# Second batch's score stacks copied inside SBUF, its pieces cut by ScalarE and VectorE, and all engine orders rewritten

## The chip, the cores and the metric

The kernel runs on one core of a Trainium2 chip. The metric is the time of one execution on the device in microseconds (us). Before the change three executions took 1351.9, 1354.87 and 1353.01 us, median 1353.01. A profiled execution took 1353.93 us.

## The reference, cut to what matters

Eight sequences ("batches") of 512 tokens with 256 features pass through four blocks, each of the form `x = x + layernorm(block(layernorm(x)))`:

```python
c_kv = x @ W_kv_down                                  # attention, 16 heads of 16
k_rope = rotary(c_kv @ W_k_rope); q_rope = rotary(x @ W_q_rope)
k, v, q = c_kv @ W_k_up, c_kv @ W_v_up, x @ W_q
scores = (q . k per head + q_rope . k_rope) / sqrt(48), causal softmax, @ v, @ W_o
h = bitlinear(x, w_fc) + gate * (x @ v.T @ fast_b.T @ u.T)   # first dense block
y = bitlinear(relu(h) ** 2, w_proj)
z = conv(x @ W_in)                                    # mixer: 32 channels of decaying sums
num = cumsum(p_w * cos(k_val * theta)), cumsum(p_w * sin(k_val * theta)); den = cumsum(p_w)
y = silu(combine(num / den, q_raw)) @ W_out
y = relu(x @ W1 + b1) @ W2 + b2                       # second dense block
```

All is float32. The products of q and k are taken in bfloat16: q and k are each cut into three bfloat16 pieces whose sum is the float32 value, and six products of pieces are summed.

## The kernel before, in words

Work is cut into named items of four chains: `a` (attention), `d` (the dense blocks, and the projections that feed the mixer), `m` (the mixer) and `p` (preparing weights, once). `a1.S.0` stands for item `S`, number 0, of chain a in batch 1. The chains of neighbouring batches overlap: while batch 1 is in its attention, batch 0 is in its first dense block and then starts its mixer. `MERGE` is a table of numbers that says, per engine, how many items of which chain come next; it is the whole order of an engine. `BANKS` gives each result its PSUM bank in TensorE's order. Every engine runs its order strictly, and waits on semaphores.

The steps of attention that matter here: `ckv`, `q`, `k`, `qr`, `kr`, `v` are projections of the normalized input xT. `base` adds the causal mask to the rotary part of the scores. `S` is one unit of scores (of 40 in a batch): TensorE multiplies two "stacks" (L983), VectorE adds the base and finds the row minimum (L1486), ScalarE takes the exponential (L1241). `T` transposes the unit on TensorE (L991), ScalarE copies it out of PSUM (L1248; for batch 0 every second one VectorE, L1415). `PV` multiplies with the values (L1009), `OT` transposes the output back (L1018). Head group g uses units 10g to 10g+9 and stack g mod 2, so group 2's stack can be loaded only when TensorE has done unit 9, and group 3's when it has done unit 19.

A stack holds 96 partitions of pieces of q (and 96 of k), with each head's 16 features on its own 16 partitions. Pieces come out of the projections with another placement, so the stacks are filled by DMA, all of them issued by SyncE (SP):

- Batch 0: ScalarE casts q from PSUM (L1223), VectorE takes the rest (L1454), ScalarE casts the rest (L1227, item `cast`), VectorE takes what is left as the third piece (L1461). The pieces lie in `hid`, and per group 12 DMAs of 64 KB copy them SBUF to SBUF into the stack (L666).
- Batches 1 to 7: ScalarE casts, VectorE takes the rest (L1422), and GpSimd casts the rest and subtracts (L794, L796). Four DMAs of 384 KB write the pieces to a `scratch` in HBM (L722, item `pieces`), and per group six DMAs read them back (L672).

The first dense block: `fxT` and `zxT` transpose normalized tokens, `fc` (eight products, L905) and `fproj` (four, L914) are the matrix products, `fystats`, `zstats`, `fnorm`, `znorm` the layernorms, in which GpSimd takes the power -0.5 (L785) between two ScalarE passes (L1180, L1171). `z.2`, `z.0`, `z.1` are the projections for the mixer; `z.0` is convolved on VectorE (L1431), stored to HBM `values` (L734) and read back spread over the partitions (`kv`, L741). The mixer's `turn` (L1548) and `frac` (L1558) on VectorE write the halves of a `ring` of 8 slots; `fold` (L1303), `cos` (L1307), `sin` (L1310) on ScalarE; `scan` (L1567) and `mix` (L1576) on VectorE; `gather` (L1077) on TensorE. `frac` number 1 writes half slot 5 of the ring.

Of the kernel before, what the change touches and what calls it, by code (L numbers as in the profile page):

```python
# [67 lines left out]
def attention_items(b):  # L68

    if b == 0:  # L70
        items = ["ckv", ("q", 0), ("cast", 0), ("k", 0), ("cast", 1), "qr", ("group", 0), ("q", 1), ("cast", 2), "kr", ("k", 1), ("cast", 3)]
# [1679 lines left out]
```

## Time and profile before

| what | value |
|---|---|
| median of three executions | 1353.01 us |
| profiled execution | 1353.93 us |
| its span in the trace | 1352.1 us |
| TensorE (PE) busy | 1197.1 us, 89% |
| VectorE (DVE) busy | 1117.4 us, 83% |
| ScalarE (ACT) busy | 1055.3 us, 78% |
| GpSimd (POOL) busy | 253.3 us, 19% |
| DMA of 64 KB, SBUF to SBUF (batch 0) | 48 of them, 2.7 us to landing |
| DMA of 384 KB to scratch | 28 of them, 4.8 us |
| stack loads from scratch (192, 128 and 64 KB) | 168 of them, median 4.2 us |

The span begins with the first instruction, 1.8 us of the execution lie around it. Busy time is a share of the whole; what a change is worth is read where it sits, which is here from 109 us (the projections of batch 1) to about 230 us (the end of its attention).

### The profile page before, as it was taken

Reading aid. Unit: us, or ns where it says so; the run is one execution under the profiler, and the core shown is the slowest. Engines: PE = TensorE matmul, PEld = TensorE weight load, DVE = VectorE, ACT = ScalarE, POOL = GpSimd, SP = SyncE. Lnnn points to the kernel's source line nnn. Section 1 sums busy time; section 2 is a strip of 40 time slices with the busy share of each in tenths; the row PEclk is TensorE's granted clock in tenths of the full one; section 3 lists DMA queues with packets and bytes.
Section 4 is the critical chain, followed back from the end, with each engine's and each line's share of the span. In section 5 each row is a group of like instructions: output and inputs, shape, how many; then the busy total and the mean of one; then the engine's idle time right before and its main releaser. Section 6 shows DMA issues by size and latency. Waiting matters only on the chain.

```text
span 1352.1 us, 23241 instructions
## 1 busy us (share of the span) xinstructions
PE 1197.1 (89%) x8060; PEld 771.1 (57%) x8060; DVE 1117.4 (83%) x2343; ACT 1055.3 (78%) x2105; POOL 253.3 (19%) x245
## 2 busy tenths in 40 slices
PE   5999995899899999998999999999899988973867
PEld 2774764466565754675656664666565764641444
DVE  2983489999699979899889997999889998899930
ACT  5775799678978989799958989698969988648542
POOL 3952000310031004200131101401131001111011
PEclk9799996999999999999999999999999999986979
DMA  4603241514024125310451131612333131023000
GB/s 141 186 18 92 42 135 39 122 35 136 32 77 103 25 63 150 87 36 21 135 125 50 30 112 39 148 24 65 103 90 75 24 114 46 32 63 95 16 16 16
DMA packets 73171, 100.07 MB, mean 74 GB/s; under 512 B 10960, under 2 KB 45920, under 8 KB 73056
## 3 DMA queue, kind: packets, MB, share of 16 engines
q1 hardware_dynamic: 73056, 98.59, 27.1%
q8 instruction: 66, 1.08, 0.3%
q14 instruction: 49, 0.40, 0.1%
HBM read 71.29 MB, written 24.12 MB: 71 GB/s over the span
## 4 chain that ended last, share of the span: by engine, by line
PE 48%; DVE 22%; ACT 18%; issue 8%; POOL 2%; SPq 1%; DMA 1%; DVEq 0%; POOLq 0%; ACTq 0%
PE ps L905 17%; PE ps L914 13%; DVE work L1567 7%; PE ps L991 5%; DVE work L1486 4%; PE ps L1009 4%; ACT work L1241 3%; PE ps L983 3%; PE ps L1077 2%; ACT xnd L1180 2%; DVE work L1558 2%; ACT work L1248 2%; ACT xnd L1171 1%; DVE work L1548 1%; DVE work L1576 1%
## 5 line engine op out<-in xcount | busy, mean ns | idle before, releaser
L1567 DVE TENSOR_TENSOR_SCAN work<-work 128x512 f32<-128x512 f32 x256 | 307.8, 1234 | 28.4 <-ACT work L1307 26.8
L1241 ACT ACTIVATE work<-work 128x384 f32<-128x384 f32 (+3 forms) x512 | 266.4, 564 | 38.5 <-DVE work L1486 37.9
L785 POOL TENSOR_TENSOR later_norms<-later_norms,singles 128x2 f32<-128x2 f32 x112 | 104.7, 939 | 864.8 <-ACT xnd L1180 583.3
L1486 DVE CUSTOM_DVE_ANT_0 work<-ps,work 128x384 f32<-128x384 f32 (+3 forms) x512 | 224.7, 486 | 35.7 <-PE ps L983 31.6
L991 PE MATMUL ps<-ident,work 128*128 128x128 f32 x1280 | 199.9, 280 | 24.1 <-ACT work L1241 20.0
L991 PEld LDWEIGHTS ps<-ident,work 128*128 128x128 f32 x1280 | 150.4, 144 | 71.9 <-issue 46.8
L1248 ACT COPY work<-ps 128x512 f32<-128x512 f32 x300 | 171.7, 579 | 2.8 <-PE ps L991 2.7
L1576 DVE TENSOR_TENSOR work<-work 128x1024 f32<-128x1024 f32 x128 | 158.4, 1238 | 4.7 <-DVEq L1400 0.2
L983 PE MATMUL ps<-work 96*128 96x384 bf16 (+3 forms) x512 | 122.7, 308 | 2.4 <-DVE hid L1510 1.1
L905 PE MATMUL ps<-led_xTd,wf 128*128 128x512 f32 x256 | 118.1, 611 | 3.9 <-issue 3.0
L914 PE MATMUL ps<-wf,hid 128*128 128x256 f32 x512 | 116.1, 387 | 4.5 <-issue 4.5
L914 PE MATMUL ps<-wpr,hid 128*128 128x256 f32 x512 | 117.1, 385 | 3.2 <-issue 2.9
L905 PE MATMUL ps<-led_xTd,wfc 128*128 128x512 f32 x256 | 116.8, 598 | 0.9 <-DVE work L1486 0.6
L914 PEld LDWEIGHTS ps<-wf,hid 128*128 128x128 f32 x512 | 98.7, 195 | 21.0 <-issue 7.2
L914 PEld LDWEIGHTS ps<-wpr,hid 128*128 128x128 f32 x512 | 96.7, 192 | 18.2 <-issue 5.0
L1009 PE MATMUL ps<-work 128*32 128x128 f32 x2560 | 93.7, 285 | 10.7 <-ACT work L1248 9.5
L1303 ACT ACTIVATE work<-work 128x1024 f32<-128x1024 f32 x64 | 67.2, 1058 | 33.4 <-DVE work L1558 33.3
L1558 DVE SCALAR_TENSOR_TENSOR work<-work,smalls 128x512 f32<-128x512 f32 x128 | 91.2, 756 | 2.2 <-ACT work L1298 0.7
L1009 PEld LDWEIGHTS ps<-work 128*32 128x32 f32 x2560 | 68.7, 113 | 37.3 <-issue 34.0
L1077 PE MATMUL ps<-work,sel 128*32 128x512 f32 x512 | 65.3, 630 | 20.3 <-DVE work L1576 20.3
L905 PEld LDWEIGHTS ps<-led_xTd,wf 128*128 128x128 f32 x256 | 48.3, 195 | 60.9 <-issue 59.7
L905 PEld LDWEIGHTS ps<-led_xTd,wfc 128*128 128x128 f32 x256 | 46.5, 190 | 52.6 <-issue 48.9
(185 smaller groups left out, 1925.4 us busy)
## 6 DMA issues: line engine op xcount, KB each, us to landing
work<-values SPq DMA_DIRECT2D x64, 256.0 KB, 3.1
work<-ratios SPq DMA_DIRECT2D x64, 256.0 KB, 3.3
scratch<-work SPq DMA_DIRECT2D x28, 384.0 KB, 4.8
work<-scratch SPq DMA_DIRECT2D x56, 192.0 KB, 4.0
work<-scratch SPq DMA_DIRECT2D x56, 128.0 KB, 4.2
x_in<-x SPq DMA_DIRECT2D x8, 512.0 KB, 6.3
values<-work SPq DMA_DIRECT2D x16, 256.0 KB, 2.7
ratios<-work SPq DMA_DIRECT2D x32, 128.0 KB, 2.8
```

The lines of the kernel that those rows point to most:

```text
L785: g_.tensor_tensor(rstds[chain][:, tokens], spreads[chain][:, tokens], power[:, tokens], ALU.pow).then_inc(*rstd.one)
L905: i = mm(dst, l, r, start=j == 0, stop=j == len(pairs) - 1)
L914: i = mm(ps[:, bank(b, name), tt % 2 * D:(tt % 2 + 1) * D], lhs[:, j, tt * P:(tt + 1) * P], rhs[:, j, :], start=j == 0, stop=j == n_k - 1)
L983: i = mm(out_of(b, name)[:, at:at + nk], stack[0:SROWS, hg % 2, 0, j, qt * P:(qt + 1) * P], stack[0:SROWS, hg % 2, 1, j, 0:nk], start=True ...
L991: i = tr(ps[:, bank(b, name), t * P:(t + 1) * P], sc[:, n % 4, t * P:(t + 1) * P], ident[:])
L1009: i = mm(ps[32 * j:32 * j + 32, bank(b, f"PV{hg}"), qt * P:(qt + 1) * P], v_all[:, v0:v0 + 32], pt[:, (hg * UNITS + u) % 6, at + t * P:at ...
L1241: i = s_.activation(part_of, part_of, ACT.Exp, scale=-1.0, bias=nmax[:, row:row + 1])
L1248: s_.copy(pt[:, n % 6, 0:nk], out_of(b, name)[:, 0:nk]).then_inc(*drains(b, name))
L1486: i = v_.tensor_tensor_reduce(sc[:, n % 4, at:at + nk], out_of(b, name)[:, at:at + nk], base_of(qt), -SCORE_SCALE, BIG, ALU.add, ALU.min, ...
L1558: i = v_.scalar_tensor_tensor(ring[:, SIN_HALF[r], m, :], kvr[:, slot, :], turns[:, r, m:m + 1], whole[:, COS_HALF[r], m, :], ALU.mult, AL ...
L1567: v_.tensor_tensor_scan(ring[:, at, m, :], pwr[:, slot, :], ring[:, at, m, :], 0.0, ALU.mult, ALU.add).then_inc(*scanned.one)
L1576: v_.tensor_tensor(both, both, qc[:, half * MH:(half + 1) * MH], ALU.mult).then_inc(*mixed.one)
```

## The change

`EARLY = 2` sets how many batches take the path of batch 0; before it was one. So in batch 1 the item order of q and k becomes that of batch 0, the second and third piece of q and k are made by ScalarE (`cast`) and VectorE in place of GpSimd, `pieces` is gone (four writes of 384 KB), and the stacks come by 48 DMAs of 64 KB from SBUF in place of 24 loads from HBM. The pieces lie in the ring's slots 5 to 7, which the mixer of batch 0 uses next: `frac` 1 of batch 0 waits for all 48 DMAs. The rest of k lies in the second half of `x2`. `MERGE` and `BANKS` are rewritten as a whole for all batches.

```diff
+EARLY = 2
 def attention_items(b):
-    if b == 0:
+    if b < EARLY:
         items = ["ckv", ("q", 0), ("cast", 0), ("k", 0), ("cast", 1), "qr", ("group", 0), ("q", 1), ("cast", 2), "kr", ("k", 1), ("cast", 3)]
     else:
         items = ["ckv", ("q", 0), ("q", 1), ("pieces", 0), "qr", ("k", 0), ("k", 1), ("pieces", 1), "kr"]
...
 MERGE = {
     "pe":
-        "a8 p2 a2 p4 a28 p a10 p a9 p a13 p a4 p a22 p a5 p a2 p2 a6 p a14 d a d a d7 a8 d a6 d a10 d a5 d a d2 "
...
+        "a4 p2 a6 p4 a25 p a4 p a9 p a11 p a18 p a16 p a p a9 p2 a5 p a15 d a2 d9 a8 d a10 d a10 d a10 d2 a11 d3 "
...
-        first_pieces = [hid[:, 3 * k:3 * k + 3, :].bitcast(BF16).rearrange("p a (b t) -> p (a b) t", t=T)
-                        .rearrange("p (c s) t -> p c s t", s=3) for k in range(2)]
+        places = [[hid[:, 3 * k:3 * k + 3, :].rearrange("p a t -> p (a t)") for k in range(2)],
+                  [ring[:, 5:8].rearrange("p a m t -> p (a m t)")[:, 3 * k * T:3 * (k + 1) * T] for k in range(2)]]
+        first_pieces = [[w.bitcast(BF16).rearrange("p (c s t) -> p c s t", c=DC, s=3) for w in pair] for pair in places]
...
-        first_rest = [rest, hid[:, 6:8, :]]
+        first_rest = [[rest, hid[:, 6:8, :]], [rest, x2[:, 1].rearrange("p t d -> p (t d)").rearrange("p (c t) -> p c t", c=DC)]]
...
             def load_group(b, hg):
-                if b == 0:
+                if b < EARLY:
                     for kind in range(2):
-                        need(sp, third_piece, 0, 2 * (hg // 2) + kind + 1)
+                        need(sp, third_piece, b, 2 * (hg // 2) + kind + 1)
...
-                if item in ("q", "k") and b:
+                if item in ("q", "k") and b >= EARLY:
                     pieces, pick = (q_pieces, (1, 2)) if item == "q" else (k_pieces, (1, 0))
...
                     need(dve, rounded, b, r + 1)
+                    if b == 0 and r == 1:
+                        for i in range(2):
+                            need(dve, first_stacked[i], 1, first_stacked[i].per_batch)
```

ScalarE at the start of batch 1's attention, beside the layernorms of batch 0's first dense block. The two passes L1171 (after: L1172) on xnd are `fnorm` 0 and 1, L1164 (L1165) copies `fxT` out of PSUM, L1234 (L1235) copies `v`. Before:

```order
L1180 ACTIVATE xnd,later_norms<-x,singles 128x256 x4
L1223 CAST work<-ps 128x512 x2
L1171 ACTIVATE xnd<-x,later_norms 128x256 x2
L1230 CAST work<-ps 128x512 x2
L1164 COPY led_xTd<-ps 128x2x256
L1171 ACTIVATE xnd<-x,later_norms 128x256 x2
L1234 COPY work<-ps 128x32x16
L1164 COPY led_xTd<-ps 128x2x256
L1234 COPY work<-ps 128x32x16
L1263 ACTIVATE hid<-ps,singles 128x512 x7
```

After:

```order
L1172 ACTIVATE xnd<-x,later_norms 128x256 x2
L1224 CAST work<-ps 128x512
L1228 CAST work<-xna 128x512
L1231 CAST work<-ps 128x512
L1228 CAST work<-x 128x512
L1224 CAST work<-ps 128x512
L1165 COPY led_xTd<-ps 128x2x256
L1228 CAST work<-xna 128x512
L1231 CAST work<-ps 128x512
L1172 ACTIVATE xnd<-x,later_norms 128x256 x2
L1165 COPY led_xTd<-ps 128x2x256
L1228 CAST work<-x 128x512
```

`fnorm` 0 stands ahead of q, and four casts (L1228) are new; `fnorm` 1 stands behind three of them and both of k's casts.

TensorE before the mixer's projections of batch 0 in the middle of batch 1's attention. L897 (L898) on xnd is the second half of `zxT`, L1058 (L1059) is `z.2`, L905 (L906) on wz is `z.0`; L991 is `T`, L983 `S`. Before:

```order
L991 MATMUL ps<-ident,work 128x128 x4
L983 MATMUL ps<-work 128x384
L983 MATMUL ps<-work 128x128
L991 MATMUL ps<-ident,work 128x128 x4
L897 MATMUL ps<-ident,xnd 128x128 x4
L1018 MATMUL ps<-ident,work 128x128 x4
L983 MATMUL ps<-work 128x384
L983 MATMUL ps<-work 128x128
L991 MATMUL ps<-ident,work 128x128 x4
L983 MATMUL ps<-work 128x256 x2
L1058 MATMUL ps<-led_xTd,wzs 32x132 x8
L905 MATMUL ps<-led_xTd,wz 128x512 x2
```

After:

```order
L992 MATMUL ps<-ident,work 128x128 x4
L1010 MATMUL ps<-work 32x128 x16
L984 MATMUL ps<-work 128x256 x2
L992 MATMUL ps<-ident,work 128x128 x4
L984 MATMUL ps<-work 128x512
L992 MATMUL ps<-ident,work 128x128 x4
L984 MATMUL ps<-work 128x512
L898 MATMUL ps<-ident,xnd 128x128 x4
L1059 MATMUL ps<-led_xTd,wzs 32x132 x8
L906 MATMUL ps<-led_xTd,wz 128x512 x2
```

Before, `z.0` comes when TensorE has sent units S 0 to 18 and T 0 to 14; after, S 0 to 21 and T 0 to 17.

VectorE where the mixer of batch 0 begins. L1548 (L1549) is `turn` 0, L1558 (L1562) `frac` 0; each pair of L1486 (L1487) rows is one part of a unit of scores. Before:

```order
L1548 TENSOR_SCALAR work<-work,smalls 128x512 x2
L1486 ISA work<-ps,work 128x256
L1486 ISA work 128x1
L1486 ISA work<-ps,work 128x256
L1486 ISA work 128x1
L1486 ISA work<-ps,work 128x512
L1486 ISA work 128x1
L1486 ISA work<-ps,work 128x512
L1486 ISA work 128x1
L1486 ISA work<-ps,work 128x512
L1486 ISA work 128x1
L1558 SCALAR_TENSOR_TENSOR work<-work,smalls 128x512 x2
```

After:

```order
L1487 ISA work<-ps,work 128x384
L1487 ISA work 128x1
L1487 ISA work<-ps,work 128x128
L1487 ISA work 128x1
L1549 TENSOR_SCALAR work<-work,smalls 128x512 x2
L1487 ISA work<-ps,work 128x256
L1487 ISA work 128x1
L1487 ISA work<-ps,work 128x256
L1487 ISA work 128x1
L1562 SCALAR_TENSOR_TENSOR work<-work,smalls 128x512 x2
```

`turn` 0 moved from behind unit 28 to behind unit 27, and `frac` 0 from behind unit 32 to behind unit 28. ScalarE's first mixer instruction, `fold` 0, moved from behind unit 32 to behind T 25.

## Rows read from the trace of the kernel before

**Rows 1.** Busy time by stretch: start:end, length, each engine, clock, DMA share, GB/s.

```profile
122.40:139.00 16.60, 16.33 (x49) 7.59 (x48) 7.87 (x18) 5.49 (x9) 1.37 (x1) 1.00 0.90 210
139.00:163.30 24.30, 23.66 (x187) 19.77 (x187) 10.21 (x41) 18.40 (x42) 1.40 (x2) 1.00 0.16 33
163.30:186.00 22.70, 20.39 (x217) 14.14 (x216) 17.01 (x61) 21.10 (x50) 1.40 (x2) 1.00 0.32 71
186.00:204.00 18.00, 14.79 (x149) 9.85 (x147) 17.14 (x53) 17.74 (x31) 0.00 (x0) 1.00 0.53 175
204.00:230.50 26.50, 15.64 (x138) 10.72 (x138) 23.48 (x45) 25.25 (x41) 1.01 (x1) 0.61 0.14 44
```

**Rows 2.** Waits of TensorE, 122 to 186 us: total, times, longest.

```profile
PE ps L897 <- ACT xnd L1171: 2.1, 1, 2.1
PE ps L991 <- ACT work L1241: 0.6, 2, 0.4
PE ps L983 <- DMA work<-scratch: 0.3, 1, 0.3
```

**Rows 3.** In order of time, batch 1's projections: start, length, engine, what, [idle before].

```profile
118.90 0.66 PE L897 MATMUL ps<-ident,xnd 128*128 128x128 f32 x4
...
122.42 12.25 PE L905 MATMUL ps<-led_xTd,wfc 128*128 128x512 f32 x28
...
117.40 0.91 ACT L1171 ACTIVATE xnd<-x,later_norms 128x256 f32<-128x256 f32 x2 [1.72 <-POOL later_norms L785]
...
120.08 0.91 ACT L1171 ACTIVATE xnd<-x,later_norms 128x256 f32<-128x256 f32 x2
```

**Rows 4.** Batch 0's second cast and third piece, by line: ns min/median/max.

```profile
L1227 ACT CAST hid<-xna x2: 603/611/619, 24.9 to 32.2; 128x512 bf16<-128x512 f32 x2
...
L1461 DVE TENSOR_TENSOR hid<-hid x2: 694/853/1012, 29.5 to 37.5; 128x512 bf16<-128x512 f32 x2
```

**Rows 5.** Batch 0's stack DMAs: SyncE's time for one issue in ns; us to landing.

```profile
L666 SPq DMA_DIRECT2D work<-hid x48: 547/594/754, 26.5 to 71.6; - x48
...
DMA to landing us min/median/max: 2.4/2.7/7.5
```

**Rows 6.** TensorE in order of time: a PV, unit 19, two transposes.

```profile
174.14 1.09 PE L1009 MATMUL ps<-work 128*32 128x128 f32 x32
175.16 0.39 PE L983 MATMUL ps<-work 96*128 96x256 bf16 x2
175.39 0.60 PE L991 MATMUL ps<-ident,work 128*128 128x128 f32 x4
...
176.05 0.60 PE L991 MATMUL ps<-ident,work 128*128 128x128 f32 x4
```

**Rows 7.** SyncE in order of time, the first stores and loads of the mixer.

```profile
180.52 0.34 SPq L734 DMA_DIRECT2D values<-work  x1
181.97 2.62 SPq L745 DMA_DIRECT2D ratios<-work  x4
184.64 2.58 SPq L741 DMA_DIRECT2D work<-values  x4
```

**Rows 8.** VectorE in order of time, start of the mixer, and one unit of ScalarE.

```profile
189.68 0.88 DVE L1548 TENSOR_SCALAR work<-work,smalls 128x512 int32<-128x512 f32 x2
...
197.10 1.41 DVE L1558 SCALAR_TENSOR_TENSOR work<-work,smalls 128x512 f32<-128x512 f32 x2
...
190.39 0.91 ACT L1241 ACTIVATE work<-work 128x256 f32<-128x256 f32 x2
191.20 0.57 ACT L1248 COPY work<-ps 128x512 f32<-128x512 f32 x1
```

**Rows 9.** A stretch of the start with its clock, and TensorE's wait ahead of it.

```profile
35.00:40.00 5.00, 5.00 (x17) 4.12 (x17) 4.01 (x9) 2.87 (x4) 5.00 (x6) 0.50 0.73 187
...
33.91 3.65 PE L1122 MATMUL ps<-work 16*128 16x256 f32 x8 [2.07 <-ACT work L1352]
```

**Rows 10.** Waits from 230 us to the end: total, times, longest.

```profile
ACT work L1303 <- DVE work L1558: 33.3, 18, 5.8
```

More of the change, by code:

```diff
@@ L73, in attention_items @@
         items = ["ckv", ("q", 0), ("q", 1), ("pieces", 0), "qr", ("k", 0), ("k", 1), ("pieces", 1), "kr"]
-    items += [("v", 0), ("v", 1), ("base", 0), ("base", 1), ("base", 2), ("base", 3), "fetch"] + [("group", 0)] * (b > 0) + [("group", 1)]
+    items += [("v", 0), ("v", 1), ("base", 0), ("base", 1), ("base", 2), ("base", 3), "fetch"] + [("group", 0)] * (b >= EARLY) + [("group", 1)]
     after = b + 1 < B
@@ L480, in sandwich_kernel @@
         third_piece = signal("third_piece", 2 * DC)
-        pieces_sent = signal("pieces_sent", 4, 16, 4 * (B - 1))
+        pieces_sent = signal("pieces_sent", 4, 16, 4 * (B - EARLY))
         n_stack = 2 * 2 * len(RUNS)
-        stacked = [signal(f"stack{i}_loaded", n_stack, 16, n_stack * (B - 1)) for i in range(2)]
-        first_stacked = [signal(f"first_stack{i}_loaded", 0, 16, 2 * 2 * SROWS // HD) for i in range(2)]
+        stacked = [signal(f"stack{i}_loaded", n_stack, 16, n_stack * (B - EARLY)) for i in range(2)]
+        first_stacked = [signal(f"first_stack{i}_loaded", 2 * 2 * SROWS // HD, 16, EARLY * 2 * 2 * SROWS // HD) for i in range(2)]
         exped = signal("exped", ALL)
@@ L666, in load_group @@
                             sp.dma_start(stack[k * HD:(k + 1) * HD, i, kind].rearrange("p j t -> p (j t)"),
-                                         first_pieces[kind][hg % 2 * 64:hg % 2 * 64 + 64, hg // 2, s, :]).then_inc(*first_stacked[i].one)
+                                         first_pieces[b][kind][hg % 2 * 64:hg % 2 * 64 + 64, hg // 2, s, :]).then_inc(*first_stacked[i].one)
                     return
@@ L716, in do @@
                     load_x(b + 1)
-                if item == "pieces" and b:
+                if item == "pieces":
                     need(sp, third_piece, b, (n + 1) * DC)
@@ L724, in do @@
                 if item == "group":
-                    if n < 2 and b:
-                        need(sp, pieces_sent, b - 1, 4)
+                    if n < 2 and b >= EARLY:
+                        need(sp, pieces_sent, b - EARLY, 4)
                     if n >= 2:
@@ L1222, in do @@
                     is_filled(act, b, f"q{n}")
-                    s_.copy((q_pieces if b else first_pieces[0])[:, n, 0, :], out_of(b, f"q{n}")).then_inc(*first_piece.one)
-                if item == "cast" and b == 0:
+                    s_.copy((q_pieces if b >= EARLY else first_pieces[b][0])[:, n, 0, :], out_of(b, f"q{n}")).then_inc(*first_piece.one)
+                if item == "cast":
                     c, kind = n // 2, n % 2
                     is_drained(act, b, f"{'qk'[kind]}{c}")
-                    s_.copy(first_pieces[kind][:, c, 1, :], first_rest[kind][:, c, :]).then_inc(*second_piece.one)
+                    s_.copy(first_pieces[b][kind][:, c, 1, :], first_rest[b][kind][:, c, :]).then_inc(*second_piece.one)
                 if item == "k":
                     is_filled(act, b, f"k{n}")
-                    s_.copy((k_pieces if b else first_pieces[1])[:, n, 2, :], out_of(b, f"k{n}")).then_inc(*first_piece.one)
+                    s_.copy((k_pieces if b >= EARLY else first_pieces[b][1])[:, n, 2, :], out_of(b, f"k{n}")).then_inc(*first_piece.one)
                 if item == "v":
@@ L1450, in do @@
                     copied(b, "ckv", ckv, out_of(b, "ckv"))
[L1451 removed]
+                if item in ("q", "k") and b < EARLY:
                     kind, of = ("q", "k").index(item), (0, 2)[item == "k"]
[L1453 to L1454 removed]
+                    need(dve, first_piece, b, 2 * n + kind + 1)
+                    v_.tensor_tensor(first_rest[b][kind][:, n, :], out_of(b, f"{item}{n}"), first_pieces[b][kind][:, n, of, :], ALU.subtract
                                      ).then_inc(*drains(b, f"{item}{n}"))
[L1456 removed]
+                if item == "q" and b >= EARLY:
                     split(b, "q", n, q_pieces[:, :, 0], 0)
[L1458 removed]
+                if item == "cast":
                     c, kind = n // 2, n % 2
                     need(dve, second_piece, b, n + 1)
[L1461 removed]
+                    v_.tensor_tensor(first_pieces[b][kind][:, c, (2, 0)[kind], :], first_rest[b][kind][:, c, :], first_pieces[b][kind][:, c, 1, :],
                                      ALU.subtract).then_inc(*third_piece.one)
@@ L1466, in do @@
                     rotate(b, "qr", qrope, T // 2)
-                if item == "k" and b:
+                if item == "k" and b >= EARLY:
                     split(b, "k", n, k_pieces[:, :, 2], DC)
```

46 lines of the change are left out of this document (20 added, 26 removed), and 75 rows, old and new, of the table MERGE.

## The prediction

> **What bounds the kernel now.** I read the page's busy shares first (the table above): TensorE 89%, VectorE 83%, ScalarE 78%. No engine stands out enough to be the only bound, so I asked for busy time by stretch over the place of the change [rows 1]. Three regimes show. From 122.4 to 139 us TensorE is full (16.33 of 16.60 us) with the `fc` products while VectorE works 7.87 us and ScalarE 5.49. From 139 to 163.3 TensorE is full (23.66 of 24.30) and ScalarE has 5.9 us to spare. From 163.3 to 230.5 ScalarE is full: 21.10 of 22.70, 17.74 of 18.00 and 25.25 of 26.50 us, 64.1 of 67.2; VectorE joins it from 186 us (17.14 of 18.00), and TensorE has 10.9 us idle in the last stretch and its granted clock is 0.61 there, so it runs at the lower of its two levels, 1.2 GHz, for most of it. So an early microsecond is gained only where TensorE idles before 163 us, and a late one only if ScalarE and VectorE get their work sooner. Third view, TensorE's waits from 122 to 186 us [rows 2]: 2.1 us for the second half of `zxT`, 0.6 us for exponentials, 0.3 us for a stack load. The last is all that batch 1's trip through HBM costs in waiting: the first unit of scores stands behind seven of eight `fc` products anyway. The change's headline step is thus worth 0.3 us, and the rest must come from what the order makes of it.
>
> **The change part by part.**
>
> *Pieces.* Four casts go to ScalarE and four subtractions to VectorE; eight instructions leave GpSimd. From batch 0's rows [rows 4] they cost 4 x 0.61 = 2.4 us on ScalarE and 4 x 0.85 = 3.4 us on VectorE (bounds 4 x 0.69 and 4 x 1.01). They lie in 113 to 123 us. TensorE has its projections to do there and both engines have gaps, so the cover is TensorE; if it were gone, the 3.4 us would count. One thing sticks out: `fnorm` 0 no longer waits for GpSimd (1.72 us, [rows 3]) as it moves ahead of q, but `fnorm` 1 now stands behind three new casts and k's second cast. I lay out ScalarE: `fxT` 0 is ready at about 119.4 (TensorE does the same products as before up to it, 118.90 + 0.5), then its copy 0.5, cast 0.5, k 0.5, `fnorm` 1 0.8, which ends near 121.8; before, the pass started at 120.08 and ended near 120.9. TensorE needs 0.5 for the transposes, ScalarE 0.6 for the copy, so the first `fc` starts at about 123.1 instead of 122.42 [rows 3]: a loss of 0.7 us, bounds 0 and 1.5.
>
> *Stacks.* SyncE issues 48 copies of 0.594 us (28.5 us) in place of 24 loads and four stores [rows 5]. Group 0: the third piece of q is there at about 116, of k at about 118.5; six issues each (3.6 us) end near 122.5, landed 2.7 us later, 125. The group 1 copies end near 130, landed 133. TensorE wants the first unit at about 139. Group 3 may be issued when unit 19 is done; 12 x 0.594 + 2.7 = 9.8 us later it is there. TensorE has 14 to 16 us of listed work between units 19 and 30 (T 16 to 26 and S 20 to 29 at 0.66 a pair, three `PV` of 1.02 [rows 6], `zxT`, the `z` products and two `query` products of four matmuls, 0.44 each by [rows 3]), so about 5 us of slack. I cost the stacks at nothing, the cover being TensorE's own work; what goes is the 0.3 us. The Trainium skill, page "DMA: Bandwidth & Descriptors", section "Rules for kernel authors", speaks against this edit: many small transfers should be joined into a large one, and under 64 KB it is mostly overhead. The trace has both kinds: a 64 KB copy lands in 2.7 us, a load from scratch in 4.2 at the median (the table), so the rule holds for SyncE's time and not for the latency that is waited for here; by the rule the slack of 5 us at unit 30 is where it would bite.
>
> *The added wait.* `frac` 1 of batch 0 waits for the last of the 48 copies. Before, `frac` 1 ran at 197.10 [rows 8]; unit 19 was done near 175.4 [rows 6], and the copies would be in by 185.2. Slack 12 us: nothing. Behind it in VectorE's queue stand `turn` 2 and units 33 on, so past that point each microsecond would count in full.
>
> *The order from 123 to 175 us.* `fproj` products now stand ahead of T 0, behind unit 8, T 9 and T 13, and the second `zxT` comes three units later. A filler of 3.5 us stands wherever TensorE would need fresh exponentials. I take the waits of [rows 2] as gone: -2.1, -0.6, -0.3. Bounds: all kept, 0; all gone, -3.0. With the 0.7 lost ahead this puts TensorE 2.3 us ahead at `z.0`, but `z.0` has three more units and a `PV` in front, 3 x 0.66 + 1.02 = 3.0 us [rows 6]. `z.0` is therefore 0.7 us later in absolute time (bounds 0 and 2).
>
> *From `z.0` to the end of batch 1's attention.* ScalarE decides [rows 1]. It has done three units more when `z.0` comes: 3 x 1.28 = 3.8 us (0.81 from start to start and 0.47 for the copy's part, [rows 8]) of the work that filled it until 230 us, taken from its idle 5.9 us before 163. That is the upper end of the gain. Against it: `values` are stored at 180.52 and `kv` is issued at 184.64 [rows 7], when that store has landed; the 2.62 us of `ratio` issues in between were hidden by the landing, so moving `kv` ahead of them gains nothing. With `z.0` 0.7 later, `kv` lands at about 188.5. VectorE now reaches `turn` 0 one unit earlier and some 2 us ahead, at about 186.5. It waits 2 us, with unit 28 behind it, and behind that `frac` 0, for which ScalarE waits at `fold` 0. If that wait is paid in full, the gain is 3.8 - 2.0 = 1.8 us. I take about the middle of 1.8 and 3.8: -2.9 us at the `gather`. This includes the 2.3 above and is not added to it.
>
> *The start.* TensorE waits 2.07 us at L1122 and runs at 0.50 of its clock from 35 to 40 us [rows 9]. The copy that frees it has the same work in front on ScalarE; q's cast now stands first and waits for TensorE until about 20.9 instead of starting at 19.6, and about as much idle further on goes. I take 0; bounds -3.5 (that stretch at the upper level) and +1.5.
>
> *Batches 2 to 7.* Single items change places with a neighbour. One kind of wait alone, ScalarE's for `frac`, comes to 33.3 us there in 18 places [rows 10]; which of them an exchange shortens or lengthens can't be read from the trace. I take 0; bounds -8 (a quarter of that row gone) and +4 (an eighth more).
>
> Sum: -2.9 us against the profiled execution's 1353.93. That execution lies 0.9 above the median of the runs, so I set the sum against the median: 1353.0 - 2.9 = 1350.1 us.
>
> **The rivals.**
>
> *R1, the exchanges pay in all batches.* If the exchanges save 1 us in each of the batches 2 to 7, as the one wait of 2.1 us [rows 2] suggests they can, -2.9 - 6 gives 1344 us. For it: the 33.3 us of [rows 10] are still there to be taken. Against: TensorE's 1197.1 us of work fill 89% of the span (the table), and a wait of ScalarE costs only where TensorE or VectorE then waits in turn.
>
> *R2, the gain is given back at `turn` 0.* If `kv` is waited for 2 us and ScalarE's head start is 2 us only (TensorE fed it no faster, because `fproj` 0 stands ahead of T 0), the attention ends when it did: 1353 us. For it: VectorE and ScalarE are both full there, and `z.0` is later.
>
> *R3, slower: the mixer starts late.* Place: `turn` 0 on VectorE, with the softmax of units 28 to 39 queued behind. Price: if the waits of [rows 2] stay, `z.0` comes 3.0 + 0.7 us later, `kv` lands near 191.5, VectorE stands from 188.5 to 191.5, and TensorE idles 3 us longer in a stretch where its clock is already at 0.61, which adds about 1: 1353 + 4 = 1357 us. It decides from the point where `kv` lands more than about 5 us behind VectorE's arrival. For it: the order is tight there. Against: it needs both the waits to stay and the head start not to be there.
>
> **How the numbers follow.** This kernel's three executions spread over 3 us, so 0.2% (2.7 us) is about what can be told from no change: faster is below 1350.3, slower above 1355.7. Forecast 0.45, its own range 1348.5 to 1352 (1.8 to 3.8 us, and the start's and the exchanges' small change); R1 0.20; R2 0.20; R3 0.15. Faster: about six tenths of the forecast and R1, 0.27 + 0.20 = 0.47. Within: the rest of the forecast and R2 but for 0.02, 0.18 + 0.18 = 0.36. Slower: R3 and that 0.02, 0.17. The range reaches into R1 and R3 and takes the start's bound of 3.5: 1343.5 to 1356.
>
> **What the profile after would show.** Right: the first `fc` near 123, the first unit of scores near 139, no wait of TensorE above 1 us between 125 and 172; VectorE idle 1 to 3 us before L1549 near 187 to 189; no wait at L1562 for the copies; the attention of batch 1 over 2 to 4 us ahead of the 230.5 us at which ScalarE's full stretch ended [rows 1]. Wrong: a wait at unit 30 for the stack, a wait of `frac` 1 for the copies, TensorE idle ahead of `fc` by over 2 us, or a start that differs by over 2 us at 100 us. If batch 1's attention ends as forecast and the end of the program doesn't keep the shift, the exchanges in batches 2 to 7 are what I valued wrongly.

## The result, and the profile after

The changed kernel takes 1356.72 us (median of 14 runs, 1352.76 to 1362.06), the kernel before 1353.70 in the runs taken beside it. The ratio is 1.0022, its 95% interval 1.0013 to 1.0031: slower by 3.0 us (1.8 to 4.2), where I had forecast 2.9 less. The profiled execution took 1356.33 us, its span 1354.5, with a mean granted clock of 0.958.

The same five stretches as in [rows 1], in the changed kernel:

```profile
122.40:139.00 16.60, 15.12 (x41) 6.84 (x39) 8.78 (x13) 8.55 (x15) 0.00 (x0) 1.00 0.34 108
139.00:163.30 24.30, 24.20 (x211) 19.37 (x210) 13.66 (x55) 18.51 (x42) 1.39 (x2) 1.00 0.10 33
163.30:186.00 22.70, 21.36 (x207) 15.40 (x204) 15.41 (x56) 20.11 (x48) 1.39 (x2) 1.00 0.19 60
186.00:204.00 18.00, 15.89 (x153) 10.31 (x151) 17.79 (x54) 17.94 (x33) 0.00 (x0) 1.00 0.61 194
204.00:230.50 26.50, 14.05 (x138) 9.90 (x138) 24.01 (x46) 25.72 (x41) 1.01 (x1) 0.74 0.13 38
```

TensorE is fuller from 139 to 186 us (45.56 us in place of 44.05) and emptier ahead of it. Its waits from 110 to 186 us, in the columns of [rows 2]:

```profile
PE ps L906 <- ACT xTa L1160: 1.2, 1, 1.2
PE ps L898 <- ACT xnd L1172: 0.8, 1, 0.8
PE ps L906 <- issue: 0.7, 1, 0.7
PE ps L1059 <- ACT led_xTd L1165: 0.7, 1, 0.7
PE ps L992 <- ACT work L1242: 0.6, 1, 0.6
```

The 2.1 us for `zxT` and the 0.3 us for a stack load of [rows 2] are gone. At `fc`, where [rows 3] has 122.42, ScalarE and (last line) TensorE now read:

```profile
118.63 0.62 ACT L1228 CAST work<-x 128x512 bf16<-128x512 f32 x1 [0.88 <-DVE x L1455]
119.16 0.58 ACT L1224 CAST work<-ps 128x512 bf16<-128x512 f32 x1
121.58 0.58 ACT L1165 COPY led_xTd<-ps 128x512 f32<-128x512 f32 x1 [1.85 <-PE ps L898]
122.07 0.62 ACT L1228 CAST work<-xna 128x512 bf16<-128x512 f32 x1
122.59 0.59 ACT L1231 CAST work<-ps 128x512 bf16<-128x512 f32 x1
123.06 0.91 ACT L1172 ACTIVATE xnd<-x,later_norms 128x256 f32<-128x256 f32 x2
...
125.41 10.97 PE L906 MATMUL ps<-led_xTd,wfc 128*128 128x512 f32 x25 [0.72 <-issue]
```

That is 3.0 us later than before, though TensorE had been 1.1 us ahead at 100 us. Most of it is the clock, read in this view of busy time of TensorE, clock, DMA share and GB/s:

```profile
96.00:100.00 4.00, 3.20 (x36) 1.00 0.02 4
100.00:108.00 8.00, 6.32 (x20) 0.57 0.00 0
108.00:112.00 4.00, 2.75 (x16) 1.00 0.01 2
```

From 100 to 108 us the granted clock averages 0.57; for most of it TensorE runs at the lower of its two levels, 1.2 GHz. The mixer's start, beside [rows 7] and [rows 8]:

```profile
181.53 0.34 SPq L735 DMA_DIRECT2D values<-work  x1
183.56 2.52 SPq L742 DMA_DIRECT2D work<-values  x4
186.13 2.89 SPq L746 DMA_DIRECT2D ratios<-work  x4
```

```profile
189.41 0.88 DVE L1549 TENSOR_SCALAR work<-work,smalls 128x512 int32<-128x512 f32 x2
190.88 1.41 DVE L1562 SCALAR_TENSOR_TENSOR work<-work,smalls 128x512 f32<-128x512 f32 x2
```

`z` is stored 1.0 us later than before and `turn` 0 starts 0.3 us earlier: with `kv` ahead of `ratio` the load is issued 2.0 us after the store, where 4.1 had passed. I compared the two traces further by matching instructions: the k-th one of the same source line, its start after less its start before, with the median over 40 us. These landmarks stand at 0.0 at 240 us and -0.2 at 440, then +2.3 at 560, +0.2 at 720, -0.6 at 800, +1.8 at 880, +3.2 at 1000 and +2.4 at 1320. So the loss does not arise in batch 1.

### The profile page after: what moved, and what is told of

The parts are those of the page before. It is cut to its first block, busy times and chain, and to the rows that moved or that the text cites. A ratio compares the mean times of both kernels' runs of the same rounds, so it can differ in the third digit from the quotient of the medians.

```text
span 1354.5 us, 23257 instructions
## 1 busy us (share of the span) xinstructions
PE 1195.6 (88%) x8060; PEld 769.4 (57%) x8060; DVE 1118.6 (83%) x2347; ACT 1055.5 (78%) x2107; POOL 245.5 (18%) x237
## 4 chain that ended last, share of the span: by engine, by line
PE 47%; ACT 22%; DVE 18%; issue 8%; POOL 3%; DMA 1%; SPq 0%; DVEq 0%; POOLq 0%; ACTq 0%
PE ps L906 18%; PE ps L915 11%; DVE work L1571 6%; PE ps L992 4%; ACT work L1242 4%; DVE work L1487 3%; PE ps L1010 3%; ACT xnd L1181 3%; ACT work L1249 3%; PE ps L1078 2%; PE ps L984 2%; POOL later_norms L786 2%; ACT xnd L1172 2%; PE ps L898 2%; DVE work L1562 1%
## 5 line engine op out<-in xcount | busy, mean ns | idle before, releaser
L786 POOL TENSOR_TENSOR later_norms<-later_norms,singles 128x2 f32<-128x2 f32 x112 | 101.0, 903 | 889.9 <-ACT xnd L1181 606.5
L1487 DVE CUSTOM_DVE_ANT_0 work<-ps,work 128x384 f32<-128x384 f32 (+3 forms) x512 | 224.2, 485 | 27.1 <-PE ps L984 22.9
L906 PE MATMUL ps<-led_xTd,wf 128*128 128x512 f32 x256 | 120.4, 621 | 3.6 <-issue 3.6
L906 PE MATMUL ps<-led_xTd,wfc 128*128 128x512 f32 x256 | 116.8, 599 | 2.1 <-DVE work L1487 1.1
L1562 DVE SCALAR_TENSOR_TENSOR work<-work,smalls 128x512 f32<-128x512 f32 x128 | 91.1, 755 | 2.2 <-ACT work L1299 0.7
L906 PEld LDWEIGHTS ps<-led_xTd,wf 128*128 128x128 f32 x256 | 49.3, 199 | 60.9 <-issue 60.0
L906 PEld LDWEIGHTS ps<-led_xTd,wfc 128*128 128x128 f32 x256 | 46.6, 190 | 55.2 <-issue 50.9
```

The costliest lines, as they stand in the source:

```text
L786: g_.tensor_tensor(rstds[chain][:, tokens], spreads[chain][:, tokens], power[:, tokens], ALU.pow).then_inc(*rstd.one)
L906: i = mm(dst, l, r, start=j == 0, stop=j == len(pairs) - 1)
L1487: i = v_.tensor_tensor_reduce(sc[:, n % 4, at:at + nk], out_of(b, name)[:, at:at + nk], base_of(qt), -SCORE_SCALE, BIG, ALU.add, ALU.min, ...
L1562: i = v_.scalar_tensor_tensor(ring[:, SIN_HALF[r], m, :], kvr[:, slot, :], turns[:, r, m:m + 1], whole[:, COS_HALF[r], m, :], ALU.mult, AL ...
```

## Experiments

The order of work is a table, so a kernel can take it from the kernel before in one stretch and from the changed one in another. I cut at points that every engine passes with the same items done in both tables. In the times of the kernel before the cuts lie at 113 us (batch 1's q), 242 (batch 2's q), 386 (batch 3's q), 528 (batch 4's `base`), 698 (batch 5's `S`), 843 (batch 6's q) and 990 (batch 7's q). The edit of each kernel is its row here: N is a stretch from the changed kernel's table, - one from the table of before; "new" stacks are the change's code (`EARLY = 2`), "old" is `EARLY = 1`.

```
     0    113  242  386  528  698  843  990   stacks
e1   N    N    N    N    N    -    -    -     new
e2   N    N    N    N    -    -    -    -     new
e3   -    -    -    -    N    N    -    -     old
e4   N    N    -    -    -    -    -    -     new
e5   -    N    -    -    -    -    -    -     new
e6   N    N    N    -    -    -    -    -     new
e7   N    N    -    N    -    -    -    -     new
e8   N    N    -    -    -    -    N    N     new
e9   e6 with one exchange on TensorE
e10  e6 with two exchanges at 860 us
e11  N    N    N    -    -    -    -    N     new
e12  N    N    -    -    -    -    -    -     old
e13  -    -    -    -    -    -    -    -     new
e14  e7 with e9's exchange undone
e15  N    N    -    -    N    -    -    -     old
e16  N    -    -    -    -    -    -    -     old
e17  the changed kernel with the exchanges of e9 and e10 undone
e18  N    N    -    -    N    -    -    -     new
```

Results: median, the kernel before in the runs beside it, the ratio with its interval, and the landmarks against the kernel before in us (one execution each).

```
      us       before   ratio   95%             80   240   440   560   720   880  1000  1320 us
after 1356.72  1353.70  1.0022  1.0013-1.0031  -1.1   0.0  -0.2   2.3   0.2   1.8   3.2   2.4
e1    1355.38  1354.10  1.0014  1.0001-1.0026  -0.8   0.4   0.3   2.8  -0.1   0.9   1.6   2.9
e2    1353.61  1354.10  1.0002  0.9989-1.0015  -1.5  -3.2  -3.1  -1.0  -1.9  -1.5  -1.5  -1.9
e3    1356.44  1354.10  1.0017  1.0002-1.0032   1.9   3.4   2.5   2.7   2.3   3.2   3.6   4.4
e4    1351.65  1354.10  0.9986  0.9972-0.9999  -1.5  -2.4  -3.1  -3.2  -4.6  -4.7  -4.7  -6.4
e5    1352.91  1354.84  0.9987  0.9975-0.9999   0.2  -0.3  -0.6  -0.6  -1.2  -1.2  -1.2  -1.1
e6    1350.41  1354.84  0.9970  0.9960-0.9980   1.1  -0.6  -0.8  -0.8  -2.3  -2.1  -2.1  -2.5
e7    1353.63  1354.84  0.9994  0.9984-1.0004  -1.2  -1.4  -1.3   1.0   0.9   1.1   1.1   1.1
e8    1353.83  1354.84  0.9995  0.9982-1.0008   0.1  -1.8   0.5   0.5  -1.4  -0.1   1.4   3.2
e9    1351.33  1353.52  0.9991  0.9979-1.0003  -0.6  -2.4  -2.7  -2.5  -3.5  -3.5  -3.6  -3.6
e10   1351.60  1353.52  0.9986  0.9976-0.9996  -1.7  -3.3  -3.9  -3.9  -5.4  -3.5  -3.2  -2.5
e11   1352.05  1353.52  0.9991  0.9980-1.0002  -1.4  -3.2  -3.7  -3.8  -5.2  -5.2  -5.1  -5.2
e12   1348.68  1353.52  0.9970  0.9958-0.9982  -1.5  -4.5  -4.9  -4.9  -4.9  -5.0  -5.0  -5.2
e13   1359.62  1354.20  1.0037  1.0022-1.0053   1.8   7.4   6.9   6.9   5.5   6.5   7.1   7.2
e14   1352.09  1354.20  0.9986  0.9974-0.9999  -1.4  -2.4  -3.2  -2.8  -4.3  -4.1  -3.3  -1.8
e15   1348.78  1354.20  0.9960  0.9948-0.9972   0.0  -2.3  -2.2  -2.0  -4.9  -4.8  -4.8  -5.8
e16   1352.55  1354.20  0.9989  0.9978-1.0000  -0.3   0.5  -0.2  -0.2  -0.3   0.1   0.1  -0.3
e17   1354.87  1354.37  1.0014  1.0002-1.0025  -1.4  -3.1  -3.2  -2.5  -4.6  -3.2  -1.5  -1.6
e18   1349.46  1354.37  0.9970  0.9961-0.9979   1.1   0.1  -1.5  -1.4  -2.3  -1.9  -1.9  -2.9
```

Read the landmarks by their steps, not their levels: the first 113 us of one kernel differ by some 3 us from one execution to the next. A single step isn't always the order's either. e8 loses 2.3 us between 240 and 440 and e14 2.3 between 880 and 1320, and e4 gains 1.7 behind 1000, all in stretches where they have the orders of before. So a place is credited to the order below only where several traces with the same order share the step. Some of the other steps have a cause that can be read. In e8, e1 and e13, all three with the orders of before at that place, TensorE waits for a stack's load from HBM ahead of the first scores of a batch. In e8 and then in e1 (e13's wait is 1.20 us, at 879 us):

```profile
412.52 1.04 PE L984 MATMUL ps<-work 96*128 96x512 bf16 x4 [1.83 <-DMA work<-scratch]
873.89 1.04 PE L984 MATMUL ps<-work 96*128 96x512 bf16 x4 [1.05 <-DMA work<-scratch]
```

In the trace of before TensorE's matmuls wait 0.6 us in all for such loads. e1's landmarks lose 1.1 us there and e13's 1.3. e8's lose 3.1, and its clock is down just behind (0.78 from 415 to 420 us).

### Is it batch 1 or what stands behind it? (e1 to e4)

e1: 

> The changed kernel, with its order and banks up to the end of batch 5's attention (about 875 us) and those of the kernel before from there on. Theory A (the exchanges of order between 745 and 1030 us cost the 3 us; the landmarks of the two traces lie 0.4 us ahead at 745, 1.9 behind at 880, 3.8 behind at 1000): this kernel keeps the first half of the loss, 1355.5 us beside 1353.7 of the kernel before, and the changed one at 1356.7. Theory B (the new pieces and stacks of batch 1 cost it, wherever the rest stands): 1356.7. Theory C (only the two parts together cost it: the early part brings the late orders to a bad meeting): 1353 to 1354.

e2: 

> The changed kernel up to about 745 us (the end of batch 3's mixer, the start of batch 5's attention), the orders and banks of the kernel before behind it. Theory A: 1353.3 us, the 0.4 us that the landmarks lie ahead there. Theory B: 1356.7 us. Theory C: 1353 to 1354.

e3: 

> The kernel before (one batch with stacks from SBUF, its own orders) with the changed kernel's orders and banks between 745 and 1030 us alone. Theory A: slower by 3 to 4 us, 1357 us. Theory B: no change, 1353.7. Theory C: no change, 1353.7, since the early part is missing.

e4: 

> The changed kernel with its orders up to the end of batch 1's attention alone (about 232 us: the new pieces and stacks, and the orders of batches 0 and 1), and the orders and banks of the kernel before behind it. Theory A: 1353.4 us, the 0.3 us that this part lies ahead in the trace. Theory B: 1356.7. My prediction's own term for this part would make it 1350.8.

The places named in the first three were one stretch too late (e5's text corrects it): e1 was cut at 698 us, e2 at 528, and e3 has 528 to 843. Batch 1 with its orders is faster by 0.14% (2.4 us by the medians), so theory B is out. e3 loses by itself, so theory C, by which the loss needs batch 1, is out. Between e4 and the changed kernel some 5 us are lost (4.9 by the ratios, whose intervals are apart). By the medians not all of it lies behind 745 us, as theory A had it: e2 has already lost what e4 gains, but their intervals overlap. e1 came out at 1355.4 us beside theory A's 1355.5, but its interval overlaps the changed kernel's.

### In which stretch? (e5 to e8, e16)

e5: 

> As e4 (the changed kernel up to batch 2's q at 242 us, the kernel before behind it), but batch 0's orders up to batch 1's q at 113 us are those of the kernel before too. What is left is the new stacks of batch 1 and the orders between 113 and 242 us. If the 1.2 to 1.5 us that the landmarks lie ahead at 80 to 100 us reach the end, this kernel is that much slower than e4: 1353 beside 1354.1 of before and 1351.65 of e4. If a wait takes them up (my prediction's 0 for the start), it is as e4, 1351.5. (The places in the texts of e1 to e3 were given one stretch too late: the cuts lay at batch 5's S, about 698 us, for e1, at batch 4's base, about 528 us, for e2, and at 528 and 843 us for e3.)

e6: 

> The changed kernel's orders up to batch 3's q (386 us), those of before behind it: e4 and the stretch from 242 to 386 us. Theory A, the loss of 2.4 us between 242 and 528 lies where TensorE's clock falls at 526 to 532 us, in the three profiled kernels with the new order there and in none of the others: no loss yet, 1351.5 to 1352. Theory B, it lies spread over the exchanges of batch 2: 1353.

e7: 

> e4 with the changed kernel's orders from 386 to 528 us alone put in. Theory A (the loss between 242 and 528 us lies before and at 530 us, where the clock falls for some 3.4 us): 1353.5 to 1354, and the profile shows the clock at 0.5 near 528 us. Theory B (spread, or batch 2's): under 1353, no fall there.

e8: 

> e4 with the changed kernel's orders from batch 6's q (843 us) to the end put in. Theory A (each stretch's exchanges cost by themselves; the landmarks of the changed kernel lose 2.7 us between 840 and 1000 us and gain 0.8 from there to the end): 1353.5. Theory C (they cost only together with the new orders of batches 2 to 5, by the shift those bring): as e4, 1351.6.

e16: 

> The kernel before with the changed kernel's orders up to 113 us alone. Theory A (the landmarks' 1.2 to 1.5 us at 80 to 100 us reach the end): 1.2 us faster than before. Theory B (my prediction's 0: a wait further on takes them up): within 0.4 us.

The start is small: e16's interval ends at no change, its landmarks have nothing left of it at 113 us, and e5 keeps 0.13% without it. From 242 to 386 us nothing is lost. From 386 to 528 us e7's landmarks lose 2.3 us, all between 440 and 560, as theory A said, and the changed kernel, e1 and e2 share that step (2.1 to 2.5). From 843 us on e8's lose 2.8 us from 720 to 1000, and the changed kernel (3.0) and e17 (3.1) share that one. The times agree in direction (1.2 and 1.0 us under before, in place of e4's 2.4 and e6's 4.4), but their intervals of 1.3 us either way overlap; the places rest on the landmarks. Four other kernels with the same orders to 242 or 386 us and few of the new ones behind (e4, e9, e10, e11) lie 1.5 to 2.4 us under before by the medians, so e6's 4.4 is likely the far end of that.

### One exchange and a clock (e9, e14)

```diff
 L953 MATMUL ps<-work,wkr 32x256 x8
-L960 MATMUL ps<-wvu,work 128x256 x2
-L899 MATMUL ps<-ident,xnd 128x128 x4
-L960 MATMUL ps<-wvu,work 128x256 x2
-L899 MATMUL ps<-ident,xnd 128x128 x4
+L960 MATMUL ps<-wvu,work 128x256 x4
+L899 MATMUL ps<-ident,xnd 128x128 x8
```

This is e9's edit on TensorE, and e14's is the reverse of it. (The experiments' line numbers lie one or two above the changed kernel's, where the table takes other lines.)

e9: 

> e6 (1350.4 us beside 1354.8 of before) with one exchange of the changed kernel on TensorE: batch 4's v.1 (4 matmuls of 128x256, 1 us) stands ahead of the transposes gxT.0 and not between gxT.0 and gxT.1. In the profile of e6 TensorE waits 0.36 and 0.70 us for ScalarE there, in e7's 1.48 us in one piece, and e7's clock falls to 0.5 behind it, at 530 us. Theory A (this exchange alone brings the clock's fall, since nothing stands any more between the two transposes): the profile shows the wait of 1.5 us and the clock at 0.5 for some 3.4 us behind 530 us, and the landmarks lose 1.5 to 2 us there. Theory B (the fall at 530 us comes from how busy TensorE was over the whole stretch ahead of it, with the other exchanges of 386 to 528 us): the wait moves, the clock stays at 1.00, and the landmarks lose under 0.4 us.

e14: 

> e7 (the changed kernel's orders up to 242 us and from 386 to 528 us) with one exchange undone: batch 4's v.1 stands between gxT.0 and gxT.1 again on TensorE. Theory A (the single wait of 1.5 us is needed, together with what e7's other exchanges do to TensorE ahead of it): no fall of the clock at 530 us, and the landmarks at 560 us lie 1.5 us or more ahead of e7's. Theory B (the other exchanges suffice): the clock falls at 530 us all the same, and the landmarks are e7's within 0.4.

TensorE in order of time in e7, then in e14:

```profile
523.79 1.99 PE L960 MATMUL ps<-wvu,work 128*128 128x256 f32 x8
525.62 0.60 PE L899 MATMUL ps<-ident,xnd 128*128 128x128 f32 x4
527.70 0.66 PE L899 MATMUL ps<-ident,xnd 128*128 128x128 f32 x4 [1.48 <-ACT xnd L1173]
529.16 7.08 PE L907 MATMUL ps<-led_xTd,wf 128*128 128x512 f32 x12 [0.81 <-issue]
```

```profile
523.37 0.66 PE L899 MATMUL ps<-ident,xnd 128*128 128x128 f32 x4 [0.36 <-ACT xnd L1173]
523.86 1.03 PE L960 MATMUL ps<-wvu,work 128*128 128x256 f32 x4
525.59 0.66 PE L899 MATMUL ps<-ident,xnd 128*128 128x128 f32 x4 [0.70 <-ACT xnd L1173]
527.05 5.39 PE L907 MATMUL ps<-led_xTd,wf 128*128 128x512 f32 x12 [0.81 <-issue]
```

The same twelve matmuls take 7.08 us in e7 and 5.39 in e14. The busy time of TensorE and its clock follow, in e7, in e14 and in e9. The latter two run some 1.9 us earlier there, so their windows are shifted by that and hold the same work:

```profile
525.00:530.00 5.00, 2.71 (x14) 1.00 0.22 48
530.00:535.00 5.00, 5.00 (x9) 0.66 0.69 159
```

```profile
523.08:528.08 5.00, 3.21 (x15) 1.00 0.22 48
528.08:533.08 5.00, 5.00 (x13) 1.00 0.69 159
```

```profile
523.15:528.15 5.00, 2.71 (x14) 1.00 0.27 60
528.15:533.15 5.00, 5.00 (x13) 1.00 0.75 169
```

The clock's mean is 0.66 in e7 behind a wait of 1.48 us, and the landmarks of e14 gain 1.9 us on e7's exactly there: 1.7 by the clock and 0.2 by the split wait. The fall shows in all four profiled executions that have the new orders from 386 to 528 us with this exchange (the changed kernel, e1, e2, e7), in neither of the two that have them without it (e14, e17), and not in e9, which has the exchange alone. In these seven executions, one of each kernel, it is needed and not enough. e9 has the same wait of 1.48 us and the same 2.71 of 5.00 us busy as e7, and its clock stays at 1.00: so neither of the two alone brings the fall, e9's theory B held, and its landmarks lose 0.2 us there. What else in the new orders must go with the exchange is open. Measured whole, e14 is 0.14% faster than before and e7 0.06%; their intervals overlap.

### Two exchanges at 860 us (e10, e17)

The edit of e10 on VectorE (the bias addition L1603 is `gystats.1`, the multiplication L1512 `fc.0`, L1488 with its sums the softmax of `S.0`); on TensorE and ScalarE `fc.0` moves ahead of `S.0` too:

```diff
+L1478 TENSOR_TENSOR work<-ps,mask 128x128
+L1477 COPY work<-ps 128x128
+L1478 TENSOR_TENSOR work<-ps,mask 128x128
 L1603 TENSOR_TENSOR xnd<-ps,b2r 128x512
-L1478 TENSOR_TENSOR work<-ps,mask 128x128
-L1477 COPY work<-ps 128x128
-L1478 TENSOR_TENSOR work<-ps,mask 128x128
...
-L1488 ISA work<-ps,work 128x512
-L1488 ISA work 128x1
+L1512 TENSOR_TENSOR hid<-ps,hid 128x512
```

e10: 

> e6 with two exchanges of the changed kernel at the start of batch 6's attention (855 to 880 us): VectorE's bias addition of batch 3's last half (gystats.1) stands behind batch 6's base.1, and batch 5's fc.0 stands ahead of batch 6's S.0 on TensorE, ScalarE and VectorE. Theory A (the chain VectorE, ScalarE's row sums, GpSimd's norms, ScalarE's scaling comes 1.2 us later, ScalarE takes fc.0 behind it, and VectorE waits 2.5 us for fc.0's values with batch 6's first scores behind it): the landmarks lose 1.2 us between 860 and 890 us and keep it to 1000 us. Theory B (the chain has slack, and e8 loses by exchanges further on, at 900 to 940 us): the wait of 2.5 us shows, and the landmarks are back within 0.3 us by 900.

Theory A held in the traces. Against e6 the landmarks lose 1.75 us between 860 and 880 and still 1.8 at 960. The times of e9 and e10, which differ in which exchange they have, can't tell it (0.09% and 0.14% under before). VectorE in order of time, and then ScalarE:

```profile
865.30 0.68 DVE L1603 TENSOR_TENSOR xnd<-ps,b2r 128x512 f32<-128x512 f32 x1
...
869.62 0.69 DVE L1512 TENSOR_TENSOR hid<-ps,hid 128x512 f32<-128x512 f32 x1 [2.46 <-ACT hid L1265]
```

```profile
866.01 0.51 ACT L1182 ACTIVATE x<-xnd,singles 128x256 f32<-128x256 f32 x1 [3.14 <-DVE xnd L1603]
...
867.93 1.09 ACT L1329 ACTIVATE xnd<-xnd,means,later_norms 128x256 f32<-128x256 f32 x2 [0.82 <-POOL later_norms L787]
868.93 0.67 ACT L1265 ACTIVATE hid<-ps,singles 128x512 f32<-128x512 f32 x1
```

VectorE's addition comes later, ScalarE's row sums wait 3.14 us for it, GpSimd's norms and ScalarE's scaling follow, and only then comes `fc.0`'s activation, for which VectorE waits 2.46 us with the first scores behind it. The changed kernel has the same wait (`DVE hid L1511 <- ACT hid L1264`, 2.5 us) from 862 to 905 us.

e17: 

> The changed kernel with the exchanges of two places undone: batch 4's v.1 between gxT.0 and gxT.1 on TensorE (526 us), and at 860 to 875 us gystats.1 ahead of batch 6's base.0 on VectorE and batch 5's fc.0 behind batch 6's S.0 on VectorE and ScalarE and behind S.3 on TensorE. Theory A (the places add up: 2.3 us by e7 and e14, 1.75 us by e10): no fall of the clock at 530 us, 4 us less than the changed kernel, 1352.7 beside 1353.7 of before. Theory B (what is regained is taken by the next full stretch, or by another fall of the clock): under 1.5 us less, 1355.5 or more.

Mostly a miss. The first place came back in full: no fall of the clock at 530 us, and 1.9 us on the changed kernel's landmarks between 530 and 540. The second did not: that wait fell to 1.0 us, but VectorE now waits 1.9 us in all for scores and ScalarE 4.2 us for the products of `fc`, and the landmarks move by no more than 0.1 us. The new table has `fc.1` to `fc.3` in a row there, and undoing one item of such a row didn't bring back what adding it had cost. By the ratios 1.1 us of the 3.0 is regained, within the intervals.

### The stacks or the orders? (e12, e13, e15, e18)

e12: 

> The kernel before (batch 1's stacks by way of HBM) with the changed kernel's orders up to 242 us, as far as its own pieces and stacks allow. Theory A (my prediction's mechanism: the stacks that come early are what lets TensorE run through 123 to 175 us; without them the later z.0 and turn only wait elsewhere): 0 to 1 us faster than before, against 2.4 for e4. Theory B (the orders alone do it, the stacks were never late enough to matter): 2 to 2.5 us faster, as e4.

e13: 

> The change's new code (batch 1's pieces by ScalarE and VectorE, 48 copies from SBUF, the wait of frac 1) in the orders of the kernel before, only the new items put in. Theory A (the stacks cost what e4's landmarks lie behind e12's: the casts stand ahead of fxT and delay the first fc): 0.5 to 1.5 us slower than before. Theory B (my prediction's sum: 0.7 lost at fc, 0.3 gained at the stack's wait): 0.4 slower at 140 us. Theory C (the stacks are what pays): 1 us or more faster.

The orders without the stacks are 0.30% faster than before; the stacks without the orders are 0.37% slower. In e12 it is theory B's case, at 4.1 us and so more than its 2 to 2.5. In e13 theory A's direction holds, at 5.0 us and so more than three times its upper end; where the new items stand in the old order was my choice, and no other placing was tried. TensorE at the first `fc`, in e12, in e4 and in e13:

```profile
119.88 0.60 PE L897 MATMUL ps<-ident,xnd 128*128 128x128 f32 x4
121.20 3.24 PE L905 MATMUL ps<-led_xTd,wfc 128*128 128x512 f32 x7 [0.72 <-issue]
```

```profile
120.86 0.66 PE L899 MATMUL ps<-ident,xnd 128*128 128x128 f32 x4 [0.76 <-ACT xnd L1173]
122.24 13.97 PE L907 MATMUL ps<-led_xTd,wfc 128*128 128x512 f32 x32 [0.72 <-issue]
```

```profile
123.93 0.66 PE L899 MATMUL ps<-ident,xnd 128*128 128x128 f32 x4 [1.62 <-ACT xnd L1173]
...
127.78 3.53 PE L907 MATMUL ps<-led_xTd,wfc 128*128 128x512 f32 x4 [2.33 <-issue]
```

With the new orders the pieces delay `fc` by 1.04 us, and nothing gives it back by 230 us (e12's landmarks lead e4's by 1.05 from 130 to 220, and the intervals of their times overlap). In e13's order ScalarE's last cast waits 2.21 us for VectorE with the copy of `fxT` 1 behind it. `fc` starts 5.4 us later than in [rows 3], 1.9 of them from this execution's start, and TensorE's clock falls right behind its wait of 2.33 us:

```profile
125.00:130.00 5.00, 2.67 (x6) 1.23 (x5) 1.71 (x3) 2.08 (x4) 0.00 (x0) 0.75 0.65 193
```

e15: 

> e12 (before's stacks, the changed kernel's orders up to 242 us, 4.1 us faster than before) with the changed kernel's orders from 528 to 698 us put in. Theory A (each stretch by itself; the profiles with these orders show stretches of low clock at 620 and 664 us and none at 698, and their landmarks gain 1.4 us between 560 and 720): 5 to 5.5 us faster than before. Theory B (the stretch of low clock only moves, and the end takes the rest): as e12, 4 us.

e18: 

> The changed kernel's code and orders up to 242 us and from 528 to 698 us, the rest as before: e15 with the new stacks. Theory A (the stacks cost 1.0 us at batch 0's fc, as between e12 and e4): 1.0 us above e15, 4.4 faster than before. Theory B (e13's 5.1 us at fc is their price wherever they stand): as before or slower. Theory C (free): as e15, 5.4 faster.

The orders from 528 to 698 us may gain: e15 is 0.10% under e12 by the ratios and e18 0.16% under e4, and in both pairs the intervals overlap. e15 is the fastest kernel of this study by the ratio, 0.40% (0.28 to 0.52) or 5.4 us faster than before, and 8 us under the changed kernel. Its landmarks gain 2.9 us between 560 and 720, and 1.7 of them are a stretch of low clock at 694 us that e12's trace has and e15's has not. That stretch isn't the order's: e3 and e18 have it with the new orders, and with those of before the profiles of e4, e6, e8, e10, e11, e13 and e14 gain 1.4 to 1.9 us on before's there all the same. e18, the same as e15 with the new stacks, is 0.30% faster; against e15 its landmarks lose 1.0 us between 120 and 130, as theory A said. e15's runs are only five, and its interval and e18's overlap.

e11: 

> e6 with the changed kernel's orders from batch 7's q (990 us) to the end put in. Theory A (each stretch by itself; e8's time and landmarks leave a gain of about 0.8 us for this stretch): 1349.6 beside 1354.8. Theory B (the end of the program takes no gain, its chains are full): within 0.5 us of e6.

By the landmarks neither gain nor loss: from 960 to 1240 us they move 0.2 us against e6's, and 0.4 the other way by the end, which is theory B. The times don't bear it out: by the ratios e11 lies 2.8 us above e6. Since e9 and e10 lie about as far above e6, I take e6's time as the odd one, which isn't shown.

## Why the prediction was wrong, step by step

*Pieces.* Right. I laid ScalarE out item by item and had `fc` 0.7 us later; e12 against e4 measures 1.04, within my bounds of 0 and 1.5.

*Stacks, and the added wait.* Right that neither is waited for. The issues took 0.594 us at the median and landed in 2.6 us, and no wait for a stack or for the copies at L1562 appears. The rule on small transfers that the prediction names (the Trainium skill, "DMA: Bandwidth & Descriptors", "Rules for kernel authors") therefore did not bite: what the stacks cost, they cost on ScalarE and VectorE and not in transfers. But the 0.3 us at which I put the trip through HBM is that of one trace. In other executions a later batch waits 1.05 to 1.83 us for such a load (e1, e13, e8); I had no term for that.

*The order from 123 to 175 us.* Right: the 2.1 us are gone in every kernel with the new orders to 242 us. I had credited the order with it (the `fproj` products in front, `zxT` three units later) and not the stacks, and e12 bears that out: it has the old stacks and the gain. e12's text calls early stacks my prediction's mechanism, which the prediction doesn't say.

*`z.0` to the end of batch 1's attention.* The size fits, -2.9 us forecast, -2.4 in e4 (its interval reaches from 0.1 to 3.8 faster), but in part by luck, since two pieces inside it were wrong. I said that moving `kv` ahead of `ratio` gains nothing because the store's landing hides it; the load now follows the store by 2.0 us and not by 4.1, so the landing had hidden at most half. And VectorE did not wait at `turn` 0, where I had 2 us. No run has this move alone, so what the earlier load is worth isn't shown. The profiled execution of the changed kernel hides the gain, since its clock fell at 100 us; e4, with the same orders up to 242 us, has 1.00 there and is 2.4 us ahead at 240.

*The start.* Right at 0: e16's 1.5 us by the ratio has an interval that ends at none, and its landmarks keep nothing.

*Batches 2 to 7.* This is the step that failed. I set the exchanges at 0 with bounds of -8 and +4, and they cost about 5 us (3.0 slower with them, 2.4 faster without, e4; from both intervals I estimate 2.7 to 7.1, and my +4 lies inside that). The changed kernel's landmarks show where: +2.5 from 440 to 560 us, -2.1 to 720, +3.0 to 1000 and -0.8 to the end. That is 2.6 of the 5, and where the rest lies is open. A part goes with the clock: over all its executions the changed kernel's mean clock is 0.9571 and e4's 0.9592, which at 0.6 us for 0.001 (below) comes to an estimated 1.3 us. Inside the loss, one place has a cause that was put in and taken out, the clock at 530 us; the exchanges at 860 us cost 1.75 us when put in and gave nothing when taken out; the cause of the remainder stays open. I priced the exchanges by one wait, and that wait went the other way. From 230 us on, beside [rows 10]:

```profile
ACT work L1304 <- DVE work L1562: 28.7, 17, 5.7
```

It fell by 4.6 us while the kernel became slower. R3's result came true (1357 us), not its mechanism: the mixer started early, with no wait at `turn` 0. My last sentence had named the case, that batch 1 comes out as forecast and the end doesn't keep it, but had given it no chance of its own; the rivals had one for exchanges that pay everywhere, R1, and none for exchanges that cost. The stated range also ended at 1356 us, below the 1357 of my own R3.

## What to carry to other kernels

A change that comes with a new order is two changes: build the old code in the new order and the new code in the old one before crediting either. Value exchanges by their chain (who is queued behind the moved item, on each engine in turn), and where only the sum of many is at stake, widen the range rather than write 0. Compare two traces by matched instructions, and trust a step that several traces with the same order share, since a single execution moves by more than such a change is worth.
